# A hybrid block on one core: mixed expert tiles make both up halves first, and the pieces of every turn stand in a new order

## The chip, the cores and the metric

The kernel runs on one core of a Trainium2 chip. The metric is the time of one execution on the device in microseconds, the median of several runs; lower is better. The core's engines are TensorE (PE in the rows; its weight loads are PEld), VectorE (DVE), ScalarE (ACT) and GpSimd (POOL). SyncE (SP) issues most of the transfers, GpSimd issues the rest, and each engine works through its own instruction list in order and waits at semaphores for the others.

## The reference

The input is 16 sequences of 512 tokens with 256 channels. Four residual parts follow one another. Only the shape of the work matters here:

```python
x = x + attn_a(layernorm(x))     # RWKV: time mix, wkv recurrence over 512 steps, channel mix 256-1024-256
x = x + ffn(layernorm(x))        # 8 experts, top 2 of each of 1024 rows: 256-1024-256, gelu
x = x + attn_b(layernorm(x))     # causal conv of 4 taps, two gates, gated recurrence, out product, RMS norm
x = x + ffn(layernorm(x))
...
# in attn_a, on its own layer norms xn and xn2 (mixed with the step before, "lx")
k, v, r = mix_k @ w_key, mix_v @ w_value, mix_r @ w_recept
out = wkv(exp(time_decay), time_first, k, v)                  # log-safe running sums
x = x + out * sigmoid(r) @ w_output
x = x + sigmoid(fmix_r @ f_w_recept) * (square(relu(fmix_k @ f_w_key)) @ f_w_value)
# in ffn
xs = xf[tok]; h = gelu(ragged_dot(xs, w1, tokens_per_expert)); ys = ragged_dot(h, w2, tokens_per_expert)
out = zeros.at[tok].add(ys * w[order][:, None]) + bias
```

The experts take `x.reshape(1024, ...)` in shape only for the scores; only the first 1024 rows of tokens (two sequences) go through them.

## The kernel before

Each of the 16 sequences is a batch of its own, held as 4 chunks of 128 tokens. The program is a row of turns, `turn_first`, `turn_0` to `turn_16`. In turn i batch i is in its time mix (`transposes_in`, `keys`, `value_columns`, `recept_columns`, the scans on VectorE, `outputs`, `transposes_mid`), batch i-1 in its channel mix (8 `channel_key`, 8 `channel_value`, `receptances`), and an earlier one p in its recurrence (`transposes_rec`, `gate_products`, `rec_products`). `ORDER` says which batch the recurrence takes p-th, and `REC_TURN` in which turn. The experts' work is cut into 40 tiles of 128 rows, 20 for each of the two passes; `tile_in`, `tile_up`, gelu and `tile_down` of tile n stand at `TILE_AT` of the turns. 32 tiles have one expert. The other eight (7, 10, 13, 16, 22, 26, 29, 33, `MIXED`) have two experts of 64 rows each. For these TensorE makes the hidden rows with the 64 rows as the weights (`two_up`, L2055, in halves a and b), ScalarE copies them to `hid_rows` (`rows_of_two`, L1155), TensorE turns them over (`two_turn`, L2062), gelu goes over them (`gelu_of`, L1164), and `two_down` (L2071) multiplies by the second weights, two experts at a time. The bank `bank_e` is shared by all of these.

What stands on each engine, and in which order, is written out by hand: each engine has its own functions with the names of the turns, and the calls in them set the order. Turns 5 to 7 share one generic function `turn(i)` on each engine. No scheduler changes this.

Weights of a tile come through SyncE's queue: `load_expert(n)` issues w1 (L482, 1 MB) and w2 (1 MB), with the tile's expert read from `table` into a register (L479), and `load_mixed_w2` issues the four pieces of 512 KB of a mixed tile (L486), two for each half, as its up halves end. The same queue stores finished batches (`store`, L534) and loads new ones (`load_x`, L453). GpSimd's queue carries `keep1` (L669), `keep2` (L685), `keep3` (L706), `residual` (L729) and the indirect transfers `gather` (L755), `picking` (L764) and `scatter_tokens` (L738); between them GpSimd makes the row norms, a power (L638) and a scaling of four chunks (L642): `norm1`, `norm2`, `norm3` of a batch are what `transposes_in`, `transposes_mid` and `transposes_rec` (all L1902) read. Other lines in the rows: L1913 is `channel_key` and `gate_products`, L1992 `channel_value`, L1920 `outputs`, `receptances` and `rec_products`, L1190 the halving of `wo` on ScalarE, L1050 the exponentials of `decay_exps`, L3145 the merge of the experts' rows on VectorE, L3041 and L3051 the last norm of a recurrence, and L3167 its residual sum.

Of the kernel before, what the change touches and what calls it, by code (L numbers as in the profile page):

```python
# [11 lines left out]
B, T, D = 16, 512, 256  # L12
# [136 lines left out]
def hybrid_kernel(nc, x, vecs, bias_row, gamma_row, w_key, w_value, w_recept, w_output, f_w_key, f_w_recept,  # L149
                  f_w_value, w_r_t, w_i_t, w_out_t, expert_weights, expert_indices, w1, w2, out):  # L150
    ctx = ExitStack()
    with ctx:
# [110 lines left out]
        hid_rows = sb("hid_rows", [P, T])  # L263
# [183 lines left out]
        def _(sp):  # L447
# [45 lines left out]
            def load_expert(n):  # L493
# [43 lines left out]
            def load_next(i, place):  # L537
                n = TILE_AT.get((i, place))
                if n in MIXED:
                    load_mixed_w2(n)  # L540
                if n is not None and n + 1 < 2 * NT and (n + 1) % NT:
                    load_expert(n + 1)

            def turn(i):
                late = [p for p in LATE if REC_TURN[p] + 1 == i]
                for b in range(2, B):
                    if i == load_turn(b) and b - NX not in [ORDER[p] for p in late]:
                        load_x(b)
                if i in NORM_TURN:
                    normalised_out(NORM_TURN.index(i))  # L550
                    if NORM_TURN.index(i) == 0:
                        sp.wait_ge(route.sem, route.count(0, "tab"))
                    load_expert(NORM_TURN.index(i) * NT)
                for place in "abcd":
                    load_next(i, place)
                    for p in late if place == "b" else []:
                        store(p)
                        if i == load_turn(ORDER[p] + NX):
                            load_x(ORDER[p] + NX)
                for p in range(B):  # L560
                    if REC_TURN[p] == i < TAIL - 1 and p not in LATE and ORDER[p] >= NB:
                        store(p)

            def tail():
                for place in "abc":
                    load_next(TAIL, place)
                for p in (13, 14, 15):
                    store(p)

            for i in range(0, TAIL):  # L570
                turn(i)
            tail()
# [10 lines left out]
        def _(pool):  # L583
# [195 lines left out]
            def turn_0():  # L779
                norm1(1)  # L780
                keep2(0)
                norm2(0)
                keep1(1)

            def turn_1():
                norm1(2)
                norm2(1)
                keep2(1)
                pool.wait_ge(weights_loaded, 7 * 16)
# [8 lines left out]
            def turn_3():  # L798
                gather(0)
                gather(1)  # L800
                keep2(2)
# [4 lines left out]
                norm2(3)  # L806
                norm3(0)
                next_gather(3, "d")
                keep2(3)
                keep1(4)  # L810

            def turn_4():
                next_gather(4, "a")
                next_gather(4, "b")
                norm1(5)
                next_gather(4, "c")
                gated_input(0)
                norm2(4)
                scaled_input(0)
                keep3(0)  # L820
# [2901 lines left out]
```

## Time and profile before

| | |
|---|---|
| median of 3 runs | 1365.28 us (1363.54 to 1368.07) |
| profiled execution | 1368.03 us, span 1366.0 us |
| TensorE busy | 1219.2 us, 89% of the span, 5812 matmuls |
| VectorE, ScalarE, GpSimd busy | 897.0, 722.5, 595.9 us |
| mean granted clock of TensorE | 0.959 |
| moved | 170.76 MB, mean 125 GB/s |

The span runs from the first to the last instruction of the profiled execution. TensorE is the busiest engine by far, so the time is read from where it stands still and from where its granted clock is below 1.00. Its clock has two levels, 2.4 GHz and 1.2 GHz; a stretch with 0.93 spent part of its time at the lower.

### The profile page before, as it was taken

Reading aid. Unit: us, or ns where it says so; the run is one execution under the profiler, and the core shown is the slowest. Engines: PE = TensorE matmul, PEld = TensorE weight load, DVE = VectorE, ACT = ScalarE, POOL = GpSimd, SP = SyncE. Lnnn points to the kernel's source line nnn. Section 1 sums busy time; section 2 is a strip of 40 time slices with the busy share of each in tenths; the row PEclk is TensorE's granted clock in tenths of the full one; section 3 lists DMA queues with packets and bytes.
Section 4 is the critical chain, followed back from the end, with each engine's and each line's share of the span. In section 5 each row is a group of like instructions: output and inputs, shape, how many; then the busy total and the mean of one; then the engine's idle time right before and its main releaser. Section 6 shows DMA issues by size and latency. Waiting matters only on the chain. (4 is left out here: it accounts for less than half of the span.)

```text
span 1366.0 us, 16873 instructions
## 1 busy us (share of the span) xinstructions
PE 1219.2 (89%) x5812; PEld 944.3 (69%) x5812; DVE 897.0 (66%) x1494; ACT 722.5 (53%) x1116; POOL 595.9 (44%) x529
## 2 busy tenths in 40 slices
PE   4699889999998989889988889899999889999981
PEld 2487677886866858568765758668768578588861
DVE  7989746566675666656879867558656555555344
ACT  3355443654734547346557657547676354463623
POOL 5336554345361443525747536545533512224142
PEclk9899999999999999999999989999999999999996
DMA  8011343547455462464230033666447544644543
GB/s 209 16 32 31 91 114 115 172 144 209 133 162 159 124 182 100 131 193 116 70 89 16 16 108 95 160 168 159 129 135 197 154 125 133 210 112 126 145 123 100
DMA packets 113029, 170.76 MB, mean 125 GB/s; under 512 B 10025, under 2 KB 86577, under 8 KB 112945
## 3 DMA queue, kind: packets, MB, share of 16 engines
q1 hardware_dynamic: 94864, 124.59, 28.6%
q0 software_dynamic: 12320, 39.86, 14.5%
q10 hardware_dynamic: 5760, 5.25, 1.1%
q8 instruction: 46, 0.75, 0.2%
q14 instruction: 39, 0.31, 0.1%
HBM read 138.20 MB, written 16.27 MB: 113 GB/s over the span
## 5 line engine op out<-in xcount | busy, mean ns | idle before, releaser
L638 POOL TENSOR_TENSOR rstd<-varis,half_neg 128x4 f32<-128x4 f32 x64 | 92.7, 1449 | 354.1 <-DVE varis L2814 188.6
L1992 PE MATMUL psum<-fwv,hid 128*128 128x256 f32 x1024 | 240.9, 384 | 0.0
L1992 PEld LDWEIGHTS psum<-fwv,hid 128*128 128x128 f32 x1024 | 194.2, 193 | 29.6 <-issue 3.3
L2033 PEld LDWEIGHTS psum<-xst,ew 128*128 128x128 f32 x1024 | 124.4, 193 | 10.9 <-ACT xst L1151 4.4
L2033 PE MATMUL psum<-xst,ew 128*128 128x128 f32 x1024 | 126.3, 277 | 4.5 <-ACT xst L1151 2.7
L2041 PE MATMUL psum<-ew,hidt 128*128 128x256 f32 x512 | 116.1, 380 | 2.1 <-ACT hidt L1164 2.1
L642 POOL TENSOR_SCALAR xhat<-rows_ring,negmean,rstd 128x256 f32<-128x256 f32 x108 | 107.8, 1009 | 18.3 <-PE psum L1902 11.2
L1064 ACT ACTIVATE hid<-psum 128x512 f32<-128x512 f32 x128 | 75.0, 594 | 71.2 <-PE psum L1913 50.8
L2041 PEld LDWEIGHTS psum<-ew,hidt 128*128 128x128 f32 x512 | 96.5, 190 | 16.8 <-ACT hidt L1164 2.6
L1913 PE MATMUL psum<-xfk_hi,fwk_hi 128*128 128x512 f32 x256 | 90.8, 436 | 8.0 <-ACT hid L1064 4.0
L1164 ACT ACTIVATE hidt<-psum 128x512 f32<-128x512 f32 x80 | 47.8, 597 | 86.8 <-PE psum L2033 79.2
L3008 DVE SCALAR_TENSOR_TENSOR space<-space,vec 128x512 f32<-128x512 f32 x90 | 62.2, 758 | 42.9 <-ACT space L1085 42.8
L1913 PE MATMUL psum<-parts,gw_hi 128*128 128x512 f32 x256 | 76.1, 421 | 15.2 <-ACT space L1105 9.9
L2919 DVE TENSOR_TENSOR_SCAN timely<-dec 128x512 f32<-128x512 f32 x32 | 37.4, 1212 | 69.4 <-ACT dec L1050 69.4
L1913 PE MATMUL psum<-parts,fwk_hi 128*128 128x512 f32 x256 | 80.7, 396 | 0.0
L755 POOL DMA_INDIRECT xs<-xf_rows,token_of_slot x40 | 50.7, 1268 | 67.5 <-PE psum L2021 53.1
L1913 PE MATMUL psum<-xfk_hi,fwk_lo 128*128 128x512 f32 x256 | 80.1, 394 | 0.0
L2827 DVE SCALAR_TENSOR_TENSOR timely<-dec,vec,xn 128x512 f32<-128x512 f32 x96 | 77.6, 866 | 1.9 <-DVE dec L2839 0.5
L1068 ACT ACTIVATE hid<-hid 128x512 f32<-128x512 f32 x128 | 77.5, 628 | 1.6 <-ACT ys L1172 0.8
L1920 PE MATMUL psum<-gwo,space 128*128 128x256 f32 x240 | 58.7, 401 | 21.4 <-DVE space L3036 16.8
L1902 PE MATMUL psum<-ident,xhat 128*128 128x128 f32 x368 | 51.7, 287 | 29.0 <-POOL xhat L642 14.9
L1014 ACT ACTIVATE xn<-psum,vec 128x512 f32<-128x512 f32 x64 | 46.2, 775 | 57.0 <-PE psum L1902 53.2
(299 smaller groups left out, 2597.9 us busy)
## 6 DMA issues: line engine op xcount, KB each, us to landing
ew<-in_w SPq DMA_DIRECT2D x64, 1024.0 KB
ew<-in_w SPq DMA_DIRECT2D x64, 512.0 KB
rows_ring<-bias_rows POOLq DMA_DIRECT2D x28, 512.0 KB, 5.6
rows_ring<-in_x SPq DMA_DIRECT2D x14, 512.0 KB, 4.6
rows_ring<-y POOLq DMA_DIRECT2D x14, 512.0 KB, 6.8
out<-rows_ring SPq DMA_DIRECT2D x14, 512.0 KB, 3.2
rows_ring<-space POOLq DMA_DIRECT2D x12, 512.0 KB, 4.7
ys_rows<-ys ACTq DMA_DIRECT2D x40, 128.0 KB
```

What stands on the lines that cost most here:

```text
L638: pool.tensor_tensor(dst, src, half_neg[:, 0:src.shape[1]], ALU.pow).then_inc(done, 1)
L642: pool.tensor_scalar(dst[:, c, :], src[:, c, :], negmean[n][:, c:c + 1], rstd[n][:, col0 + c:col0 + c + 1], ALU.add, ALU.mult).then_inc(st ...
L1064: nc.scalar.activation(hid[:, j % NHID, :], ring[f"f{j}"], ACT.Relu).then_inc(relu.sem, 1)
L1068: nc.scalar.activation(hid[:, j % NHID, :], hid[:, j % NHID, :], ACT.Square).then_inc(sq.sem, 1)
L1902: last = nc.tensor.transpose(bank_t[:, c, k * P:(k + 1) * P], src[:, k, c * P:(c + 1) * P], ident[:])
L1913: last = nc.tensor.matmul(dst, w[a][:, c, m * P:(m + 1) * P], src[b][:, c, :], start=n == 0, stop=n == len(terms) - 1)
L1920: last = nc.tensor.matmul(dst[:, k, :], src[:, c, k * P:(k + 1) * P], w[:, c, :], start=c == 0, stop=c == chunks - 1)
L1992: last = nc.tensor.matmul(rows4[:, k, :], hid[:, j % NHID, k * P:(k + 1) * P], fwv[:, j, :], start=j == 0 and k % 2 == 0, stop=j == FC - 1 ...
L2033: last = nc.tensor.matmul(bank_e[:, j * P:(j + 1) * P], ew1[:, c, at:at + P], xst[:, c, :], start=c == 0, stop=c == DC - 1)
L2041: last = nc.tensor.matmul(bank_e[:, 0:D], hidt[:, j, :], ew2[:, j, :], start=j == 0, stop=j == FC - 1)
L2827: nc.vector.scalar_tensor_tensor(dst[:, c, :], diff[:, c, :], col(m, c), xn[:, c, 0:T], ALU.mult, ALU.add).then_inc(st.sem, 1)
L3008: nc.vector.scalar_tensor_tensor(s.cv[:, c, :], s.xc[:, c, j:j + T], col(f"conv{j}", c), s.cv[:, c, :], ALU.mult, ALU.add).then_inc(conv.s ...
```

## The change

The pieces of work are the same on every engine, and so are `ORDER`, `REC_TURN`, `TILE_AT` and `MIXED`. Three things differ.

First, `hid_rows` becomes two buffers. TensorE's order at a mixed tile was up a, turn a, up b, turn b, with up b behind gelu a; it becomes up a, up b, turn a, turn b. Up b waits for the copy of half a alone, both turns wait for the copy of half b, and turn b for gelu a too.

Second, SyncE's list is written out turn by turn. `load_expert` is split in `load_first` (w1) and `load_second` (w2), and `load_mixed_w2` in `load_two_w2(n, half)`. The second weights of mixed tiles go ahead of stores, and mostly of loads of x. In a plain tile the expert's number is now read twice, once for each part, and in a mixed one once for each half. At tiles 9 and 20 the second part stands ahead of the first, at tiles 13 and 26 half 1 ahead of half 0.

Third, turns 5 to 7 get lists of their own in place of `turn(i)`, and the calls stand in a new order in all turns, on all five engines. The diff, cut to the functions that change and to some of the lists:

```diff
-        hid_rows = sb("hid_rows", [P, T])
+        hid_rows = [sb(f"hid_rows{n}", [P, T]) for n in range(2)]
...
-            def load_expert(n):
+            def load_first(n):
...
+            def load_second(n):
+                experts = uses(n) if n in MIXED else [expert_in(tile_of(n))]
                 if n:
                     sp.wait_ge(tiles_done, n)
...
-            def load_mixed_w2(n):
+            def load_two_w2(n, half_no):
                 experts = uses(n)
-                for half_no in range(2):
-                    await_step(sp, up, n, "ab"[half_no])
-                    for x, e in enumerate(experts):
-                        load_w2(two_w2[half_no][:, x], e, half_no * FC // 2, FC // 2)
+                await_step(sp, up, n, "ab"[half_no])
+                for x, e in enumerate(experts):
+                    load_w2(two_w2[half_no][:, x], e, half_no * FC // 2, FC // 2)
...
             def rows_of_two(n, half_no):
                 await_step(act, up, n, "ab"[half_no])
-                nc.scalar.activation(hid_rows[:], bank_e, ACT.Copy).then_inc(rows_up.sem, 1)
+                nc.scalar.activation(hid_rows[half_no][:], bank_e, ACT.Copy).then_inc(rows_up.sem, 1)
...
                 if half_no == 0:
                     pe.wait_ge(xst_ready, n + 1)
                 else:
-                    await_step(pe, gelu, n, "a")
+                    await_step(pe, rows_up, MIXED.index(n), "a")
...
             def two_turn(n, half_no):
-                await_step(pe, rows_up, MIXED.index(n), "ab"[half_no])
+                await_step(pe, rows_up, MIXED.index(n), "b")
+                if half_no:
+                    await_step(pe, gelu, n, "a")
```

ScalarE, start: the wait for all late weights and the halving of `wo` move ahead of `values_out(0)` and `decay_exps(0)`.

```diff
-                values_out(0)
-
-            def turn_0():
+
+            def turn_0():
+                act.wait_ge(weights_loaded, 112)
+                nc.scalar.mul(wo[:], wo[:], 0.5).then_inc(split_his, 1)
+                values_out(0)
                 decay_exps(0)
                 weight_exp(0)
                 norm_in(1)
-                act.wait_ge(weights_loaded, 7 * 16)
-                nc.scalar.mul(wo[:], wo[:], 0.5).then_inc(split_his, 1)
```

The next rows are SyncE's instructions around mixed tile 10 (turn 6), before. L482 is the first weights of the tile, L534 a store, L453 a load of x, L479 the reading of expert numbers, L486 the second weights.

```order
106 L482 DMA ew<-in_w 128x2x512
107 L534 DMA out<-rows_ring 128x4x256
108 L453 DMA rows_ring<-in_x 128x4x256
109 L479 TENSOR_LOAD table
110 L479 ISA x2
111 L479 TENSOR_LOAD table
112 L479 ISA x2
113 L486 ISA
114 L486 DMA ew<-in_w 128x4x256
115 L486 ISA
116 L486 DMA ew<-in_w 128x4x256
```

And SyncE at the same place in the changed kernel:

```order
145 L482 DMA ew<-in_w 128x2x512
146 L453 DMA rows_ring<-in_x 128x4x256
147 L479 TENSOR_LOAD table
148 L479 ISA x2
149 L479 TENSOR_LOAD table
150 L479 ISA x2
151 L486 ISA
152 L486 DMA ew<-in_w 128x4x256
153 L486 ISA
154 L486 DMA ew<-in_w 128x4x256
155 L479 TENSOR_LOAD table
156 L479 ISA x2
```

The store has gone from there, the first two transfers of second weights keep the load of x ahead of them, and the expert numbers are read again between the two halves.

GpSimd in turn 3, before. L755 gathers an expert tile's rows, L685 is `keep2(2)`, L638 with L642 are norms, L669 is `keep1(3)`; the `xhat` row at the end is `norm1(4)`.

```order
51 L744 TENSOR_TENSOR rstd<-varis,half_neg 128x8
52 L755 DMA xs<-xf_rows,token_of_slot 128x256 x2
53 L685 DMA rows_ring<-y 128x1024
54 L638 TENSOR_TENSOR rstd<-varis,half_neg 128x4
55 L642 TENSOR_SCALAR y<-rows_ring,negmean,rstd 128x256 x4
56 L669 DMA rows_ring<-bias_rows 128x1024
57 L638 TENSOR_TENSOR rstd<-varis,half_neg 128x4
58 L642 TENSOR_SCALAR xhat<-rows_ring,negmean,rstd 128x256 x4
```

GpSimd at the same place in the changed kernel:

```order
51 L894 TENSOR_TENSOR rstd<-varis,half_neg 128x8
52 L835 DMA rows_ring<-y 128x1024
53 L905 DMA xs<-xf_rows,token_of_slot 128x256 x2
54 L788 TENSOR_TENSOR rstd<-varis,half_neg 128x4
55 L792 TENSOR_SCALAR y<-rows_ring,negmean,rstd 128x256 x4
56 L819 DMA rows_ring<-bias_rows 128x1024
57 L788 TENSOR_TENSOR rstd<-varis,half_neg 128x4
58 L792 TENSOR_SCALAR xhat<-rows_ring,negmean,rstd 128x256 x4
```

`keep2(2)` now stands ahead of the two gathers; the rest is as it was.

Five more places of which the prediction speaks:

- GpSimd, turn 9: before `norm1(10)`, `picking(0, 0)`, `picking(0, 1)`, `norm3(5)`; now `picking(0, 1)` stands behind `norm3(5)`.
- GpSimd, turn 11: before `norm3(8)`, `gather(NT + 1)`, the gathers of places b and c, `keep3(7)`, `residual(7)`; now `keep3(7)` stands ahead of `norm3(8)`, and `residual(7)` ahead of the gather of place c.
- ScalarE, turn 8: before `relu_of(7, 0)` stands behind `weight_exp(8)`, now 14 calls ahead of it.
- TensorE: before `transposes_mid` of the batch stands right ahead of `rec_products` in turns 5 to 7 with nothing between them; now other work of 1.7 to 5.2 us of TensorE stands between.
- VectorE, last turn: before all 16 instructions of the merge at the end, behind `residual(15)`; now 8 of them (`merge(1, 0)`) between `recur(15)` and `mean_square(15)`.

## Rows read from the trace of the kernel before

**Rows 1.** The page, busy time by engine: us, share of the span, instructions.

```profile
PE 1219.2 (89%) x5812; PEld 944.3 (69%) x5812; DVE 897.0 (66%) x1494; ACT 722.5 (53%) x1116; POOL 595.9 (44%) x529
```

**Rows 2.** Waits of PE: total us, number of waits, longest us.

```profile
PE psum L2071 <- DMA ew<-in_w: 16.3, 5, 4.1
PE psum L1902 <- POOL xhat L642: 14.9, 7, 4.3
...
PE psum L1920 <- ACT xn L1014: 4.6, 3, 1.5
```

**Rows 3.** Stretches: length, busy us by engine, granted clock, DMA share, GB/s.

```profile
188.00:210.00 22.00, 17.85 (x89) 15.47 (x88) 11.29 (x20) 5.47 (x9) 8.58 (x5) 0.84 0.29 90
210.00:377.00 167.00, 164.46 (x856) 131.72 (x854) 105.23 (x164) 93.69 (x144) 73.00 (x60) 1.00 0.52 155
410.00:435.00 25.00, 20.57 (x109) 15.55 (x108) 10.28 (x13) 12.06 (x16) 0.43 (x1) 0.93 0.60 172
586.00:606.00 20.00, 15.88 (x91) 11.86 (x90) 12.18 (x14) 11.43 (x15) 4.51 (x4) 0.91 0.67 204
683.00:710.00 27.00, 21.78 (x91) 17.77 (x90) 19.39 (x35) 12.99 (x22) 9.91 (x12) 0.87 0.45 112
710.00:795.00 85.00, 74.51 (x305) 56.16 (x304) 70.24 (x112) 57.77 (x87) 52.29 (x37) 0.94 0.07 13
860.00:885.00 25.00, 19.84 (x81) 14.84 (x80) 9.03 (x17) 13.39 (x18) 12.82 (x12) 0.86 0.62 173
```

**Rows 4.** Timeline of 399:423, SP's queue and PE: start, us, what, idle before.

```profile
401.33 0.39 SPq L534 DMA_DIRECT2D out<-rows_ring  x1
...
404.44 3.62 SPq L486 DMA_DIRECT2D ew<-in_w  x4
...
405.01 1.94 PE L2055 MATMUL psum<-ew,xst 128*64 128x512 f32 x8
...
419.56 3.01 PE L2071 MATMUL psum<-ew,hidt 128*64 128x256 f32 x16 [3.85 <-DMA ew<-in_w]
```

**Rows 5.** Timeline of POOL, 162:193.

```profile
162.59 1.47 POOL L755 DMA_INDIRECT xs<-xf_rows,token_of_slot  x1 [7.95 <-DMA xf_rows<-ew]
...
165.78 1.04 POOL L685 DMA_DIRECT2D rows_ring<-y  x1
...
176.38 2.18 POOL L642 TENSOR_SCALAR y<-rows_ring,negmean,rstd 128x256 f32<-128x256 f32 x4 [0.22 <-POOL rstd L638]
...
183.23 9.13 POOL L642 TENSOR_SCALAR xhat<-rows_ring,negmean,rstd 128x256 f32<-128x256 f32 x4 [0.20 <-issue]
```

**Rows 6.** Timeline of POOL, 661:690.

```profile
661.70 1.12 POOL L764 DMA_INDIRECT ew<-ys_rows,slot_i  x1 [0.18 <-issue]
...
685.57 1.21 POOL L638 TENSOR_TENSOR rstd<-varis,half_neg 128x4 f32<-128x4 f32 x1
```

**Rows 7.** Timeline of POOL, 860:863.

```profile
861.11 0.89 POOL L729 DMA_DIRECT2D rows_ring<-space  x1 [5.04 <-issue]
```

**Rows 8.** Timeline of PE, 862:870.

```profile
866.48 2.08 PE L1913 MATMUL psum<-parts,gw_hi 128*128 128x512 f32 x4 [5.16 <-ACT space L1105]
```

**Rows 9.** Timeline of DVE, 1343:1366.

```profile
1352.55 0.17 DVE L3041 TENSOR_SCALAR msq<-ssq 128x4 f32<-128x4 f32 x1 [7.77 <-ACT square L1144]
...
1356.06 7.41 DVE L3145 SCALAR_TENSOR_TENSOR xf<-ew,choice_w,xf 128x256 f32<-128x256 f32 x16
```

**Rows 10.** Timeline of ACT, 27:30.

```profile
27.49 1.91 ACT L1050 ACTIVATE dec<-dec 128x2048 f32<-128x2048 f32 x1 [0.77 <-DVE dec L2914]
```

**Rows 11.** Timeline of SP's queue, 15:19.

```profile
17.02 0.72 SPq L473 DMA_DIRECT2D choice_w<-in_expert_weights  x1
```

**Rows 12.** DMA issues: transfer, KB, median us to landing.

```profile
choice_w<-in_expert_weights SPq DMA_DIRECT2D x1, 8.0 KB, 11.7
```

**Rows 13.** Timeline of PE, 40:50.

```profile
43.91 5.82 PE L1920 MATMUL psum<-wo,dec 128*128 128x256 f32 x16 [13.52 <-DVE dec L2955]
```

**Rows 14.** Critical chain, 1263:1265: start, us, step.

```profile
1263.19 1.40 PE psum L1913 x6
```

More of the change, by code:

```diff
@@ L535, in store @@
                     .then_inc(out_stored[without_experts(p) % 3], 16)
[L537 to L572, printed above, removed]
+            def turn_first():
+                pass
+            def turn_0():
+                load_x(2)
+            def turn_1():
+                pass
+            def turn_2():
+                load_x(4)
+                load_x(3)
+            def turn_3():
+                load_x(5)
+                normalised_out(0)
+                sp.wait_ge(route.sem, route.count(0, "tab"))
+                load_first(0 * NT)
+                load_second(0 * NT)
+                load_first(1)
+                load_second(1)
+                load_first(2)
+                load_second(2)
+                load_first(3)
+                load_second(3)
@@ L573, in _ @@
+            turn_first()
+            turn_0()
+            turn_1()
+            turn_2()
+            turn_3()
+            turn_4()
+            turn_5()
+            turn_6()
+            turn_7()
+            turn_8()
+            turn_9()
+            turn_10()
+            turn_11()
+            turn_12()
+            turn_13()
+            turn_14()
+            turn_15()
+            turn_16()
             for b in range(NB):
@@ new lines, in turn_6, with turn_7 @@
+            def turn_6():
+                keep3(2)
+                norm1(7)
+                gated_input(2)
+                scaled_input(2)
+                keep2(6)
+                norm2(6)
+                next_gather(6, "b")
+                keep1(7)
+                norm3(3)
+                mean_power(2)
+                next_gather(6, "c")
+            def turn_7():
+                norm1(8)
+                residual(2)
+                next_gather(7, "a")
+                gated_input(3)
+                scaled_input(3)
+                keep2(7)
+                norm2(7)
+                next_gather(7, "b")
+                next_gather(7, "c")
+                norm3(4)
+                keep3(3)
+                mean_power(3)
+                residual(3)
+                keep1(8)
@@ L987, in _ @@
             turn_4()
-            for i in range(5, 8):
-                turn(i)
+            turn_5()
+            turn_6()
+            turn_7()
             turn_8()
@@ L1882, in _ @@
             turn_4()
-            for i in range(5, 8):
-                turn(i)
+            turn_5()
+            turn_6()
+            turn_7()
             turn_8()
@@ L2759, in _ @@
             turn_4()
-            for i in range(5, 8):
-                turn(i)
+            turn_5()
+            turn_6()
+            turn_7()
             turn_8()
@@ L3674, in _ @@
             turn_4()
-            for i in range(5, 8):
-                turn(i)
+            turn_5()
+            turn_6()
+            turn_7()
             turn_8()
```

1924 lines of the change are left out of this document (1153 added, 771 removed).

## The prediction

> **What bounds the kernel now.** I read the page first. TensorE is busy 1219.2 of 1366 us [rows 1]; no other engine comes near, so the kernel loses time where TensorE stands still (147 us in all) and where its granted clock falls. Then the table of its waits: the largest named kinds that this change touches are second weights not landed (16.3 us in 5 waits), row norms from GpSimd (14.9 in 7), and copies of `xn` on ScalarE (4.6 in 3) [rows 2]. Then stretches of time, cut at the waits of 3 us and more. From 210 to 377 TensorE is busy 164.46 of 167 us at clock 1.00, so there an order has nothing to give. Right behind the waits the clock is not full: 0.84, 0.93, 0.91, 0.87, 0.86 [rows 3]. So each wait is paid twice, itself and then (1 - clock) times its stretch: 3.5 us in 188:210, 1.8 in 410:435, 1.8 in 586:606, 3.5 in 683:710, 3.5 in 860:885. The mean clock of 0.959 over the span makes that 56 us in all. Last, the timelines around each wait, to see what came last.
>
> **The change part by part.** All pieces of work stay, so what can change is waits and the clock behind them. I write the sum against the profiled execution, 1368.0 us; the median of the runs shown is 2.7 lower.
>
> *A, second weights of mixed tiles.* At tile 10 the four transfers are issued from 404.44 over 3.62 us, behind a store at 401.33 and a load of x, and TensorE starts the second half of `two_down` at 419.56 after 3.85 us of waiting [rows 4]. Between issue and landing lie 15.1 us, in which some 2.6 MB move at the stretch's 172 GB/s: these second weights (2 MB) and the load of x. Now the store is gone from there, so the queue is free some 3 us earlier, and half 0 no longer shares its wait with half 1; the last byte would land near 401.5 + 15.1 = 416.6. On TensorE, between the end of up b and `two_down` stood 6.7 us of work (two pieces of `channel_key` at 1.40 [rows 14], the turn, `receptances`); now both turns, a product of the time mix, a piece more of `channel_key` and the transposes of a middle norm stand there, 12.9 us counted from the order. That need not make `two_down` later; it makes up b earlier. So its second half wants its weights at 419.56 - 3.85 = 415.7 at the earliest, and 417.4 with the extra piece ahead: the wait goes, by a margin of only 1 us. The other mixed tiles gain alike (6.7 to 12.5 at tile 7, 6.7 to 11.1 at 13, 1.7 to 8.0 at 29, 2.7 to 7.7 at 33). Full worth: 16.3 plus four stretches like 410:435 at 1.8 of clock, 23.5. Lower bound 0, if the landing doesn't move; I take 18.
>
> *B, GpSimd in turn 3.* `keep2(2)` is issued at 165.78, behind two gathers of which the first waited 7.95 us for the experts' rows. So the norm behind it starts only at 176.38 and `norm1(4)`'s scaling at 183.23, where it takes 9.13 us [rows 5]; TensorE waits for it, idle 4.15 of 22 us with 3.5 of clock (17.85 busy at 0.84) [rows 3]. Now `keep2(2)` is ahead of the gathers. What is late next is the `y` norm's own operands, which have been there for long. -7.5.
>
> *C, GpSimd in turn 9.* 16 indirect transfers from 661.70 to 685.57 stand ahead of `norm3(5)` [rows 6], and TensorE stands idle for it, 27 less 21.78 or 5.2 us, and loses 3.5 of clock behind [rows 3], 8.7. Eight of the 16 now stand behind it, 12 us earlier. I take 6, since the middle norm and `keep2(9)` are behind those eight.
>
> *D, GpSimd in turn 11.* `residual(7)` is issued at 861.11 after 5.04 us of waiting for the transfer ahead of it [rows 7]; ScalarE's tanh of the gates waits for its landing, TensorE for the tanh, 5.16 us [rows 8], and 3.5 of clock. Now `keep3(7)` is ahead of `norm3(8)` and `residual(7)` ahead of the third gather: over 6 us earlier. -8.5.
>
> *E, ScalarE in turn 8.* `relu_of(7, 0)` behind `weight_exp(8)`: 20 us with 15.88 busy and 1.8 of clock [rows 3]. Now 14 calls earlier. -5.9.
>
> *F, middle transposes.* `rec_products` right behind `transposes_mid` waits for the copy of `xn` that empties its bank, 4.6 us in 3 waits [rows 2]. Now work of 1.7 to 5.2 us lies between. -4.6.
>
> *G, the end.* VectorE stands idle 7.77 us before 1352.55, and then has a merge of 16 instructions, 7.41 us, as the last compute [rows 9]. Eight of them (3.7 us) now fit into that idle time. -3.7.
>
> *H, the start.* ScalarE's `decay_exps(0)` ran at 27.49 [rows 10]. Now the wait for all late weights stands ahead, whose last transfer is issued at 17.02 [rows 11] and takes 11.7 us to land [rows 12]: that is 28.7, and with the halving of `wo` and the values' copy (0.6 each) the exponentials start near 30.3. Scans follow from there up to `outputs(0)`, which already waits 13.52 us for them [rows 13]. Between 0 and +3; I take +2.4.
>
> *I, new waits.* The middle transposes of batch 10 already wait, the longest of the seven (4.3) [rows 2], and stand 2.4 us of work nearer to `outputs(10)`. Gates of batches 5 to 7 stand 1.6 nearer to the products that need them; tile 9's first weights go behind its second (+1); the expert numbers are read twice on SyncE, which is idle then. +5, between 0 and 15.
>
> The sum of the named parts is -18 - 7.5 - 6 - 8.5 - 5.9 - 4.6 - 3.7 + 2.4 + 5 = -46.8. Not all of it will stay. These are chains over four engines, and where one wait goes, the next late piece shows; from 710 to 795 TensorE has 10.5 us idle and 5.1 of clock with no wait above 4.3 [rows 2, 3], which is how a tight order looks once the great waits are gone. I keep two thirds: -31, so 1337 in the profile's terms, **1334.5 as the median**.
>
> **Two rules weighed.** From 410 to 435 the DMA engines are busy 0.60 of the time [rows 3]. So they aren't full on average, and moving a store out of the way frees the queue more than the engines. The Trainium skill, page "DMA: Bandwidth & Descriptors", section "Issuing engines are not separate DMA queues", says that transfers of all issuers run on the same 16 engines and interleave; by it an earlier issue only spreads the same bytes, and A would be worth little. The trace half agrees: 0.60 busy leaves room, 15.1 us for 2.6 MB does not look like it.
>
> Four scalings by GpSimd took 2.18 us at 176.38 and 9.13 at 183.23, the same instruction on the same shapes [rows 5]. So a norm's price depends on what runs beside it. The Trainium skill, page "SBUF — State Buffer", section "A bandwidth-pool intuition that's wrong (but worth ruling out)", says that GpSimd and a VectorE operation on two ports exclude one another, one fully blocked; by that the slow scaling follows VectorE's place in the order, and a new order moves it at random.
>
> **The rivals.**
> - *Bandwidth.* Second weights land no earlier. For: 15.1 us from issue to landing at 172 GB/s, and the margin of 1 us in A. Against: 0.60 busy. A is worth 6 in place of 18, the sum -34.8, two thirds of it -23: 1345 profiled, 1342 as the median (1336 to 1350). 0.20.
> - *Nearly all is kept.* Each wait was alone in its chain. The sum itself, -47: 1321 profiled, 1318 (1311 to 1322). For: 210:377 shows that an order can run at 98% [rows 3]. 0.16.
> - *Slower: norms on GpSimd come late in the new order.* Each one that TensorE waits for costs up to 4.3 [rows 2] and some 1.8 of clock, 6.1 together. Seven did before. Against the 31 us kept it decides from five more on; seven more make +43, 1368 + 12 = 1380 profiled, 1377. For: 9.13 against 2.18, and 16 batches have three norms each. Against: B, C and D free that engine of waits. 0.13.
> - *No change.* New waits eat all that the named ones give: within 4.1 us of 1365.3. 0.08.
>
> **How the numbers follow.** The likeliest case (0.43) has its own range of 1322 to 1346. Three tenths of a per cent, 4.1 us, is about what can be told from no change. Faster: 0.43 + 0.20 + 0.16 = 0.79; same 0.08; slower 0.13. The range for 8 in 10 leaves out half of the case where nearly all is kept and the slower one: 1315 to 1364.
>
> **What the profile after would show.** A: second weights under 5 us in TensorE's waits, and full clock behind the mixed tiles; if the wait is there with the transfers issued 3 us earlier, bandwidth was the cause. B, C, D: the waits at `transposes_in(4)`, `transposes_rec(5)` and `gate_products(8)` gone; busy share in the matching stretches above 97%. G: no more than four us of merge behind the last residual sum. H: `outputs(0)` starting near 46.5. TensorE's busy time itself should fall from 1219 by 15 to 20 us, as the clock is full for longer; the mean clock near 0.97. The prediction is wrong if new waits of 3 us and more stand where none were, above all for norms from GpSimd with scalings of 6 to 9 us.

## The result and the profile after

| | before | changed |
|---|---|---|
| median | 1364.41 us (1362.59 to 1368.07, 4 runs) | 1284.51 us (1283.05 to 1289.51, 4 runs) |
| span of the profiled execution | 1366.0 us | 1281.0 us |
| mean granted clock | 0.959 | 0.979 |

The ratio is 0.9418 (95% interval 0.9385 to 0.9451): faster by 79 us, where 31 were forecast. The time lies below the range, which began at 1315.

The page of the changed kernel, head and busy times:

```profile
span 1281.0 us, 17105 instructions
...
PE 1194.1 (93%) x5812; PEld 932.4 (73%) x5812; DVE 889.7 (69%) x1494; ACT 717.9 (56%) x1116; POOL 606.5 (47%) x529
```

Against [rows 1] TensorE is busy 25 us less with the same 5812 matmuls, which is the clock, and stands idle 87 in place of 147 us. (1 - clock) times the span is 56.0 before and 26.9 after. So of the 85 us of span 60 are waits, and 25 of busy time is speed (29 by the difference of the two clock products).

TensorE's waits by releaser, the kinds that answer to [rows 2] (L2182 is L1902 of before, L2193 L1913, L2313 L2033, L2321 L2041):

```profile
PE psum L2182 <- POOL xhat L792: 13.0, 7, 3.4
...
PE psum L2321 <- DMA ew<-in_w: 2.2, 1, 2.2
...
PE psum L2313 <- DMA ew<-in_w: 0.8, 1, 0.8
PE psum L2193 <- ACT hid L1243: 0.8, 1, 0.8
...
PE psum L2193 <- ACT space L1284: 0.5, 1, 0.5
```

Not one wait at `two_down` (L2353) is left of the 16.3 us. In their place stand small ones at plain tiles. The copies of `xn` no longer appear at all. Norms from GpSimd still cost 13.0 in 7, and not at the same places.

Stretches, cut where the same pieces now lie, to hold against [rows 3]:

```profile
184.00:206.00 22.00, 19.29 (x103) 17.08 (x102) 12.84 (x22) 10.08 (x15) 8.68 (x7) 0.92 0.37 114
229.00:604.00 375.00, 372.97 (x1922) 293.59 (x1922) 249.75 (x400) 215.75 (x339) 171.00 (x143) 1.00 0.58 166
395.00:420.00 25.00, 25.00 (x151) 20.68 (x150) 17.60 (x29) 15.30 (x23) 9.65 (x10) 1.00 0.62 158
545.00:565.00 20.00, 20.00 (x115) 14.61 (x114) 13.35 (x26) 14.57 (x22) 7.63 (x9) 1.00 0.88 236
641.00:668.00 27.00, 26.22 (x121) 21.67 (x119) 23.43 (x44) 18.40 (x27) 20.80 (x19) 1.00 0.29 75
668.00:753.00 85.00, 73.61 (x300) 54.79 (x300) 78.17 (x120) 59.04 (x89) 52.94 (x37) 0.96 0.10 19
803.00:828.00 25.00, 25.00 (x126) 19.90 (x125) 16.80 (x29) 15.68 (x23) 7.94 (x6) 1.00 0.54 162
```

The first is `transposes_in(4)`: 19.29 in place of 17.85 busy. The second shows the reach of the new order: 375 us of turns 4 to 8 with two us of TensorE idle. The next two are tile 10 and turn 8, full at clock 1.00, even with the DMA engines 0.88 busy at 236 GB/s. Then turn 9; then turn 10, which is idle for as long as it was (73.61 of 85 busy, 74.51 before); then turn 11, full.

Tile 10, SyncE's queue and TensorE, against [rows 4]:

```profile
383.21 1.94 PE L2335 MATMUL psum<-ew,xst 128*64 128x512 f32 x8
...
385.34 6.45 SPq L486 DMA_DIRECT2D ew<-in_w  x4
...
388.71 1.94 PE L2335 MATMUL psum<-ew,xst 128*64 128x512 f32 x8
...
403.54 3.67 PE L2353 MATMUL psum<-ew,hidt 128*64 128x256 f32 x32
```

The second weights are issued from 385.34 over 6.45 us, the last of them after up b at 388.71, and `two_down` runs 32 matmuls in 3.67 us without a break.

GpSimd in turn 3, against [rows 5]:

```profile
152.88 1.00 POOL L835 DMA_DIRECT2D rows_ring<-y  x1
...
168.56 2.18 POOL L792 TENSOR_SCALAR y<-rows_ring,negmean,rstd 128x256 f32<-128x256 f32 x4 [0.22 <-POOL rstd L788]
...
180.69 7.22 POOL L792 TENSOR_SCALAR xhat<-rows_ring,negmean,rstd 128x256 f32<-128x256 f32 x4 [0.20 <-issue]
```

`keep2(2)` is 13 us ahead and the `y` norm 8, but the `xhat` scaling for batch 4 only 2.5 us earlier, at 180.69: it waits for its own statistics now. 2.7 of TensorE's 4.15 us stay in this profile. The size of this one wait moves between profiles of kernels with the same lists there: 1.6 in three later runs, 2.7 in three.

The end, VectorE, against [rows 9]:

```profile
1262.82 3.76 DVE L3524 SCALAR_TENSOR_TENSOR xf<-ew,choice_w,xf 128x256 f32<-128x256 f32 x8
1270.93 0.17 DVE L3420 TENSOR_SCALAR msq<-ssq 128x4 f32<-128x4 f32 x1 [4.36 <-ACT square L1323]
...
1274.45 3.75 DVE L3524 SCALAR_TENSOR_TENSOR xf<-ew,choice_w,xf 128x256 f32<-128x256 f32 x8
```

Half the merge (3.76) lies in front of the last norm, and idle time there is down from 7.77 to 4.36. The start, against [rows 13]:

```profile
45.88 4.49 PE L2200 MATMUL psum<-wo,dec 128*128 128x256 f32 x13 [13.52 <-DVE dec L3334]
```

`outputs(0)` starts 2.0 us later, as step H said.

### The profile page after: what moved, and what is told of

Read it like the earlier page. It is cut to its first block and busy times, and to the rows that moved or that the text cites. A ratio compares the mean times of both kernels' runs of the same rounds, so it can differ in the third digit from the quotient of the medians.

```text
span 1281.0 us, 17105 instructions
## 1 busy us (share of the span) xinstructions
PE 1194.1 (93%) x5812; PEld 932.4 (73%) x5812; DVE 889.7 (69%) x1494; ACT 717.9 (56%) x1116; POOL 606.5 (47%) x529
## 3 DMA queue, kind: packets, MB, share of 16 engines
q10 hardware_dynamic: 5760, 5.25, 1.2%
## 5 line engine op out<-in xcount | busy, mean ns | idle before, releaser
L788 POOL TENSOR_TENSOR rstd<-varis,half_neg 128x4 f32<-128x4 f32 x64 | 97.1, 1518 | 246.4 <-DVE varis L3193 178.1
L2313 PEld LDWEIGHTS psum<-xst,ew 128*128 128x128 f32 x1024 | 125.8, 194 | 8.2 <-issue 3.6
L792 POOL TENSOR_SCALAR xhat<-rows_ring,negmean,rstd 128x256 f32<-128x256 f32 x108 | 122.2, 1141 | 16.5 <-PE psum L2182 9.6
L2313 PE MATMUL psum<-xst,ew 128*128 128x128 f32 x1024 | 126.6, 277 | 1.4 <-DMA ew<-in_w 0.8
L2321 PE MATMUL psum<-ew,hidt 128*128 128x256 f32 x512 | 117.6, 383 | 2.9 <-DMA ew<-in_w 2.2
L2321 PEld LDWEIGHTS psum<-ew,hidt 128*128 128x128 f32 x512 | 98.0, 192 | 18.4 <-issue 3.8
L2193 PE MATMUL psum<-xfk_hi,fwk_hi 128*128 128x512 f32 x256 | 94.6, 451 | 1.8 <-ACT timely L1221 1.8
L905 POOL DMA_INDIRECT xs<-xf_rows,token_of_slot x40 | 45.4, 1134 | 92.0 <-PE psum L2301 73.1
L2193 PE MATMUL psum<-parts,fwk_hi 128*128 128x512 f32 x256 | 80.7, 396 | 0.0
L2193 PE MATMUL psum<-xfk_hi,fwk_lo 128*128 128x512 f32 x256 | 80.2, 395 | 0.0
L863 POOL TENSOR_TENSOR space<-space 128x1024 f32<-128x1024 f32 x14 | 33.3, 2379 | 88.4 <-ACT space L1294 88.4
L2182 PE MATMUL psum<-ident,xhat 128*128 128x128 f32 x368 | 50.4, 282 | 26.2 <-POOL xhat L792 13.0
L3206 DVE SCALAR_TENSOR_TENSOR timely<-dec,vec,xn 128x512 f32<-128x512 f32 x96 | 73.8, 822 | 1.5 <-DVE dec L3218 0.5
L2193 PE MATMUL psum<-parts,gw_hi 128*128 128x512 f32 x256 | 71.9, 403 | 1.3 <-ACT hid L1243 0.8
L2200 PE MATMUL psum<-wo,dec 128*128 128x256 f32 x256 | 59.5, 386 | 13.7 <-DVE dec L3334 13.5
L2182 PEld LDWEIGHTS psum<-ident,xhat 128*128 128x128 f32 x368 | 43.1, 144 | 37.4 <-issue 32.5
```

The source lines that it names most:

```text
L788: pool.tensor_tensor(dst, src, half_neg[:, 0:src.shape[1]], ALU.pow).then_inc(done, 1)
L792: pool.tensor_scalar(dst[:, c, :], src[:, c, :], negmean[n][:, c:c + 1], rstd[n][:, col0 + c:col0 + c + 1], ALU.add, ALU.mult).then_inc(st ...
L2182: last = nc.tensor.transpose(bank_t[:, c, k * P:(k + 1) * P], src[:, k, c * P:(c + 1) * P], ident[:])
L2193: last = nc.tensor.matmul(dst, w[a][:, c, m * P:(m + 1) * P], src[b][:, c, :], start=n == 0, stop=n == len(terms) - 1)
L2200: last = nc.tensor.matmul(dst[:, k, :], src[:, c, k * P:(k + 1) * P], w[:, c, :], start=c == 0, stop=c == chunks - 1)
L2313: last = nc.tensor.matmul(bank_e[:, j * P:(j + 1) * P], ew1[:, c, at:at + P], xst[:, c, :], start=c == 0, stop=c == DC - 1)
```

## The experiments

Two theories were held against each other in most of them. *Every wait stands alone*: TensorE's next late piece depends on work near by, so a wait that is taken away comes back in full, with its clock, and later ones keep their sizes. *Waits are passed on*: TensorE then comes early to the next piece, and part of the gain is given back. The second was the reason for keeping two thirds in the forecast. Times are given as ratios to the kernel before, which ran beside each; "slower than the changed kernel" means the difference of such a ratio and 0.9418, in us, and is good to 6 or 7 us.

**The mixed tiles alone** (kernel before, with up b and turn a changing places, and the queue's order; ScalarE copies half b to its buffer ahead of gelu a, and the tiles from 16 on are changed in the same way):

```diff
-                two_turn(a, 0)
+                two_up(a, 1)
                 ...
-                two_up(a, 1)
+                two_turn(a, 0)
```

and in SyncE's list, at the head of its `turn(i)`, which serves turns 0 to 15 on this engine (the store's old place at the end goes):

```diff
+                if TILE_AT.get((i, "a")) in MIXED:
+                    load_mixed_w2(TILE_AT[i, "a"])
+                for p in range(B):
+                    if REC_TURN[p] == i - 1 and p not in LATE and ORDER[p] >= NB:
+                        store(p)
```

> The kernel before, with the mixed tiles alone changed: both up halves first in two buffers, and in SyncE's queue the second weights of the mixed tile at the head of a turn ahead of the pending store and the load of x. Theory 'every wait stands alone': 16.3 us of weight waits and four times 1.8 of clock come back, 1341 to 1345 from 1364.4, and the waits behind keep their sizes. Theory 'waits are passed on': TensorE comes earlier to the next late piece, and two thirds or less of it stays, 1349 to 1356. Theory 'bandwidth': the second weights land no earlier, the waits stay above 10 us, 1358 or more.

Measured 1347.01 us, ratio 0.9853 (0.9814 to 0.9892): 20 us. From 1364.4 that is 1344.3, in the first theory's range; the interval reaches to the edge of the second's. No wait for second weights at `two_down` is left. Three of the waits that had nothing to do with the edit, as they stand in this kernel's table (two lines later in the file):

```profile
PE psum L1904 <- POOL xhat L644: 14.7, 7, 4.1
...
PE psum L1904 <- POOL hidt L644: 5.2, 1, 5.2
PE psum L1922 <- ACT xn L1016: 4.6, 3, 1.5
```

14.7, 5.2 and 4.6, as in the kernel before (14.9, 5.2 and 4.6). Only small new ones at the second turn (1.26 us, three times, for gelu) took something back. The waits speak for the first theory.

**The queue's order alone** (the second half of that diff, without the first):

> The kernel before with SyncE's order alone changed: second weights of the mixed tile at the head of a turn first, then the store, then x. If the queue's order is the cause of the weight waits: most of the 20 us of both parts together, 1346 to 1351. If the two up halves next to each other are: 1358 or more.

Ratio 0.9967 (0.9945 to 0.9989): 4.5 us. Tile 10 in its timeline:

```profile
399.54 7.73 SPq L486 DMA_DIRECT2D ew<-in_w  x4
...
404.23 1.94 PE L2057 MATMUL psum<-ew,xst 128*64 128x512 f32 x8
...
407.31 0.51 SPq L534 DMA_DIRECT2D out<-rows_ring  x1
...
418.56 3.44 PE L2073 MATMUL psum<-ew,hidt 128*64 128x256 f32 x16 [3.63 <-DMA ew<-in_w]
```

The store now stands behind the weights, half 0 is issued 4.9 us earlier than in [rows 4], and TensorE still waits 3.63 for half 1, as half 1 can only be issued after up b (404.23). It was up b's place that set the issue, not the store. Step A of the prediction had the wrong link here, with the right total. In the mixed tiles alone up b ends at the same time, but `two_down` starts 2.7 us further behind it (416.46 for 413.76), and there is no wait.

**The order of up and turn undone in the changed kernel** (the first half of the diff, backwards):

> The changed kernel with up b behind gelu a again (up a, turn a, up b, turn b), all other places as they are. By the order the work between up b and two_down falls by about 1.3 us at most. Theory 'the swap is what helps': TensorE waits again at up b or at two_down, 6 us or more, 1291 or more. Theory 'the placing of other work and the queue help, the swap hardly': within 3 us of 1284.5.

1291.71 us, ratio 0.9453 (0.9415 to 0.9491), 4.8 us by the ratios, though the two intervals overlap. The time lies at the edge of the first theory's range, its sign does not show: the profile has weight waits of 1.95 and 1.31 us back, at tiles 22 and 26, and none at 10 or 13. With the other work placed in front of `two_down`, most tiles don't need the two halves next to each other.

**Three moves on GpSimd alone** (B, C and D in the kernel before):

```diff
+                keep2(2)
                 gather(0)
                 gather(1)
-                keep2(2)
...
-                picking(0, 1)
                 norm3(5)
+                picking(0, 1)
...
+                keep3(7)
                 norm3(8)
                 gather(NT + 1)
                 next_gather(11, "b")
+                residual(7)
                 next_gather(11, "c")
-                keep3(7)
-                residual(7)
```

> The kernel before, with three moves on GpSimd alone: keep2(2) ahead of the gathers in turn 3, picking(0, 1) behind norm3(5) in turn 9, keep3(7) and residual(7) forward in turn 11. Theory 'every wait stands alone': 7.5 + 8.7 + 8.5 less what stays at transposes_in(4) (2.7 in the changed kernel) gives 22, 1342 to 1346. Theory 'waits are passed on': 10 to 15 us, 1350 to 1355, with new waits within some 30 us behind each place.

1351.57 us, ratio 0.9884 (0.9846 to 0.9921): 16 us, less than the first theory's 22. The waits at `transposes_in(4)` and `gate_products(8)` are gone; at `transposes_rec(5)` 4.1 of 5.2 us stay. GpSimd shows why:

```profile
672.97 1.95 POOL L638 TENSOR_TENSOR rstd<-varis,half_neg 128x4 f32<-128x4 f32 x1 [6.18 <-DVE varis L2814]
675.12 7.05 POOL L642 TENSOR_SCALAR hidt<-xf,negmean,rstd 128x256 f32<-128x256 f32 x4 [0.20 <-issue]
```

With the picks out of the way the norm waits 6.18 us for VectorE's statistics, and its scaling takes 7.05 us, where it took 2.27 behind the picks. VectorE is busy for 6.46 of the 7.1 us, and was for 0.2 of the 2.2. B and D came in full, C did not, and little was passed on: behind the start, every other wait of 0.3 us and more stayed within half a microsecond but for one at the second weights of tile 29, which fell from 4.13 to 2.75.

**The same three undone in the changed kernel:**

> The changed kernel with the same three GpSimd moves undone. Theory 'every wait stands alone': +17 to +22, 1302 to 1307. Theory 'waits are passed on' (a kernel freed of its waits is the more sensitive): other waits appear too, over +22. Theory 'the other lists made these moves needless': under +8.

1299.53 us, ratio 0.9502 (0.9467 to 0.9536), 11.5 us by the ratios and 16.6 by the spans. The first is in none of the three ranges, the second just under the first of them, so this run decides nothing between the theories. `transposes_in(4)` waits 7.9 us (2.7 with the moves), `gate_products(8)` 5.4, and undoing C brings a wait at another place:

```profile
650.05 1.22 PE L2193 MATMUL psum<-xfk_hi,fwk_hi 128*128 128x512 f32 x2 [4.28 <-ACT hid L1243]
```

This is `channel_key(8, 4)`. So a move may keep a different wait away than the one that it had removed in the old order.

**The last turn alone** (lists of TensorE, ScalarE and VectorE for turn 16 from the changed kernel):

> The kernel before, with the last turn alone as in the changed kernel on TensorE, ScalarE and VectorE (rec_products(14) ahead of expert tile 38, transposes_rec(15) ahead of the second half of up of tile 39, half the merge ahead of mean_square(15)). The prediction priced only the merge, 3.7 us. 'Every wait stands alone': the merge's 3 to 3.7, and the wait of 5.25 at gate_products(15) with its clock, 8 to 12 in all, 1352 to 1356 beside 1364. If only the merge counts: 1360 to 1361.

1357.07 us, ratio 0.9939 (0.9917 to 0.9961): 8.3 us. The wait of 5.25 at `gate_products(15)` is gone, and 2.7 for weights at the last tile is new.

**The last turn undone in the changed kernel:**

> The changed kernel with the last turn of TensorE, ScalarE and VectorE as before. The last turn alone gave 0.6 per cent, 8.3 us, in the kernel before. 'Every wait stands alone': +8 to +11, 1293 to 1296, with gate_products(15) waiting 5 us again. 'Passed on': under +5.

1288.23 us, ratio 0.9439 (0.9405 to 0.9472): 2.9 us by the ratios and 4.2 by the spans: under 5, as 'passed on' had it. The 5.24 are back, but the 2.2 for weights at tile 39 are gone with it.

**All named parts together, and two more moves** (`weight_exp(8)` behind `relu_of(7, 0)`, `rec_products(p)` behind `keys(i + 1)` in turns 5 to 7):

> The kernel before with everything of the earlier single runs together (mixed tiles and queue, three GpSimd moves, the last turn) and two more: weight_exp(8) behind relu_of(7, 0) on ScalarE, rec_products behind keys(i + 1) in turns 5 to 7. 'Every wait stands alone': the ratios multiply, 0.985 x 0.988 x the tail's, and 5 + 4 us for the last two, so 1305 to 1312. 'Waits are passed on': 1320 or more, with waits in places where the single runs had none.

1329.18 us, ratio 0.9722 (0.9682 to 0.9762): 38 us. The three single parts multiply to 0.968, 44 us, so the two more moves gave nothing, or took up to 6 (which the intervals don't tell from nothing), where 9 had been expected. The time lies in the range of 'waits are passed on'. In the profile the three waits of 1.54 at `rec_products` are gone, and `transposes_rec(4)`, behind them, waits 5.1 us for VectorE where it had waited 1.8, and `value_columns` waits 0.64 twice; `channel_key(7, 3)` still waits 2.6 of 3.5. Here a move made by hand on one engine, without the others' lists being fitted to it, was passed on. `channel_key(2, 0)`, far from both, waits 4.3 for 1.8, for which the trace names no releaser. It does so in the run of the last turn alone too, where `transposes_in(4)` behind it waits 2.4 less, so it belongs to neither move; what makes it vary stays open.

**The two halves of the program.** The lists of all engines and the queue were cut at turn 9: the changed ones in front and those of before behind, and the other way round. Two pieces and a load of x that had crossed the cut were put back.

> The changed kernel up to turn 8, and the lists of the kernel before from turn 9 on, on all engines and the queue (mixed tiles 22, 26, 29, 33 in the old order of up and turn). In the profiles outputs(9) starts 45 us earlier in the changed kernel, the rest comes behind. If the two halves of the program add: 1320 to 1324, and the waits behind turn 9 as in the kernel before, to 0.3 us. If late lists lose what early ones gave: 1330 or more.

1336.9 us, ratio 0.9796 (0.9759 to 0.9833): 28 us, and in the range that had been given to the rival. The profile in two stretches:

```profile
229.00:603.00 374.00, 372.11 (x1916) 292.70 (x1914) 249.17 (x400) 215.57 (x339) 169.14 (x143) 1.00 0.57 164
603.00:1300.00 697.00, 637.49 (x3047) 500.79 (x3048) 442.58 (x725) 392.82 (x617) 307.41 (x262) 0.96 0.44 122
```

Up to 603 it is the changed kernel, with 1.9 us idle from 229 on; behind, it has the waits of before, `gate_products(8)` 5.26, `rec_products(11)` 3.68, `receptances(14)` 1.82, beside one of 6.4 at the cut itself, at `transposes_in(10)`. The cut lies between `outputs(8)` and `outputs(9)`. From the one to the other, first in the kernel before, then here:

```profile
628.00:699.90 71.90, 66.48 (x307) 52.96 (x306) 55.25 (x92) 35.41 (x57) 45.42 (x41) 0.95 0.40 105
587.40:670.60 83.20, 72.24 (x315) 57.93 (x314) 55.34 (x94) 38.26 (x59) 47.26 (x41) 0.92 0.34 89
```

At `outputs(8)` this kernel is 40.6 us ahead of the kernel before (the changed one 39.7), at `outputs(9)` only 29.3. So the 11 us were lost at the cut, and behind it, from `outputs(9)` to the end, it takes 663.8 us, where the kernel before took 666.2: the late lists of before lost nothing of what the early ones gave.

> The other half: the kernel before up to turn 8, the changed lists from turn 9 on. If the halves add: 1365 less 80 plus 43, 1326 to 1331. If the early lists are a condition for the late ones: 1340 or more.

1319.66 us, ratio 0.9665 (0.9631 to 0.9699): 46 us, and 6 us under the range. Neither run hit its range, since 45 us had been put in front of the cut, where 40 lie, and nothing had been put down for the seam. The product of the two ratios is 0.9468, the ratio of the whole change 0.9418. By the spans the halves give 31.7 and 47.3 us, 79.0 of 85.1. So the halves add, but for 6 or 7 us that the seam costs.

**One engine's whole list undone.** What was open by then was which list carried the rest of the gain.

> The changed kernel with the whole list of GpSimd as in the kernel before; the other engines and the queue as changed. The three moves alone, undone, cost 11 us. If the rest of GpSimd's new order matters little: 1296 to 1300. If each engine's list carries its share of the small waits: 1305 or more.

1329.17 us, ratio 0.9738 (0.9703 to 0.9773): 44 us slower than the changed kernel. Waits for norms grow (7.3 at `transposes_in(4)`, 6.0 at `transposes_mid(12)`, 4.9 at `transposes_in(14)`, 4.6 at `transposes_rec(5)`), and 5.2 us at the second weights of tile 13.

> The changed kernel with SyncE's whole list as in the kernel before (stores and loads of x ahead of the second weights of mixed tiles). The queue's order alone gave 4.5 us in the kernel before. If the work that now lies between up b and two_down covers the late landing by itself: under +4, no wait at two_down. If not: 16 us of weight waits and their clock are back, 1300 or more.

1320.37 us, ratio 0.9671 (0.964 to 0.9703): 35 us slower than the changed kernel. TensorE's wait for second weights:

```profile
PE psum L2203 <- DMA ew<-in_w: 33.8, 8, 11.5
```

And why, at tile 10, GpSimd and SyncE's queue:

```profile
395.45 1.24 POOL L729 DMA_DIRECT2D rows_ring<-space  x1
...
403.20 0.39 SPq L534 DMA_DIRECT2D out<-rows_ring  x1
...
406.48 2.48 SPq L486 DMA_DIRECT2D ew<-in_w  x4
```

The store at 403.20 waits for the landing of `residual`, which GpSimd issues at 395.45, and load of x and second weights wait behind it, to 406.48. `two_down(10)` then stands 11.5 us. In the kernel before `residual` stood at 396.67 and the first second weights at 404.44, hardly otherwise. But there up b ended at 406.95, so half 1 could not be issued before; here up b ends at 389.57, both halves could be issued from then on, and TensorE wants them from 402.5 on. In the kernel before the queue's order cost 4.5 us. In the new order the whole old list costs 35.

**The start put back** (changed kernel, on ScalarE):

```diff
-                act.wait_ge(weights_loaded, 112)
-                nc.scalar.mul(wo[:], wo[:], 0.5).then_inc(split_his, 1)
                 values_out(0)
                 ...
                 norm_in(1)
+                act.wait_ge(weights_loaded, 112)
+                nc.scalar.mul(wo[:], wo[:], 0.5).then_inc(split_his, 1)
```

> The changed kernel with the start of ScalarE as before: the wait for the late weights and the halving of wo behind norm_in(1). The chain decay_exps(0) to outputs(0) is shorter by about 2 us and is what TensorE waits for (13.5), so 2 us faster, 1282 to 1283. If the load of the late weights is what counts: no difference.

1278.78 us, ratio 0.9373 (0.9343 to 0.9403). `outputs(0)` starts at 43.59 for 45.88. The 2.3 us are the start's; the rest of the distance in the medians is within what two sets of runs differ by.

**Three waits of middle norms covered by one piece each:**

> The changed kernel with the start of ScalarE as before, and on TensorE three of the waits that are left (transposes_mid(8), (10) and (12), 2.1, 2.9 and 3.4 us) each covered by one piece of 1.7 us that stood behind. 'Every wait stands alone': 1.7 us less at each and some clock, 5 to 7 us under the version with the start put back, near 1273. 'Passed on': the same time, since the next product waits for the norms behind the transposes.

1279.83 us, ratio 0.9364 (0.9341 to 0.9387): the same. `transposes_mid(12)` in it, TensorE:

```profile
892.34 1.07 PE L2182 MATMUL psum<-ident,xhat 128*128 128x128 f32 x8 [1.35 <-POOL xhat L792]
895.83 0.66 PE L2301 MATMUL psum<-ident,xs 128*128 128x128 f32 x2 [2.42 <-ACT ys L1351]
...
909.07 1.99 PE L2272 MATMUL psum<-fwv,hid 128*128 128x256 f32 x8 [1.82 <-ACT hid L1247]
```

Its wait fell from 3.4 to 1.35, and 2.42 came at `tile_in(25)` and 1.82 at the next `channel_value`. Passed on, as in the two hand moves above.

## Why the prediction was wrong

**What bounds the kernel** and the double price of a wait were right: beside 60 us less idle time the clock gave 25 to 29, nearly half as much again, and the 39 us of named waits had been priced with 19.5 of clock.

**A** was taken at 18 and measured 20 alone, and all weight waits went. Its mechanism was half right. In the old order the second half's issue hung on up b, not on the store; in the new one the queue decides, as the queue list of before costs 35 us there. The working from 15.1 us and 172 GB/s was off too: that rate is the mean of 410:435, and between issue and landing the engines moved 284 GB/s (below). **B** went to 0 in the old order with the one move, but in the changed kernel 2.7 of 4.15 stay, as the norm's own statistics are late next. **C** was right in the changed kernel, where the wait is gone, but the move alone gave 1 us of 5.2; it named the picks, and VectorE's statistics and a slow scaling came last right behind them. **D** held in full. **E** and **F** are gone in the changed kernel, but the one move that the prediction named for each took F's waits away only to bring another of the same size, and E's by a quarter. **G** measured 3.2 from `rec_products(15)` to the end, for 3.7. **H** was right to 0.4 us. **I** was too small in waits: new or larger ones stand at `transposes_mid(12)` 3.4, `transposes_rec(7)` 3.1, `tile_down(39)` 2.2, `transposes_mid(8)` 2.1 and `channel_key(10, 1)` 1.8 (0.7 in seven of the later runs with the same turn). The sign that was to tell that the prediction is wrong, new waits of 3 us and more, is there twice, and the kernel is faster than forecast all the same.

**The step that failed first is the sum.** It came to 47, and the span fell by 85. Even with nothing taken off it, the forecast would have been 1318, and 1284.5 lies far below that. It priced the waits that had a name, most of them of 3 us and more. Taking off start and end (30.0 and 13.0 us), the waits of 0.3 us and more at single pieces make 88 us in the kernel before, and of these the named ones 39. The other 49 stood at zero. Four of them, at `recept_columns(10)`, `gate_products(7)`, `rec_products(11)` and `gate_products(15)`:

```profile
726.92 2.40 PE L1907 MATMUL psum<-timely,wr 128*128 128x512 f32 x3 [3.20 <-ACT timely L1037]
...
800.09 1.22 PE L1913 MATMUL psum<-parts,gw_hi 128*128 128x512 f32 x2 [3.11 <-ACT space L1105]
...
1067.73 1.84 PE L1920 MATMUL psum<-gwo,space 128*128 128x256 f32 x6 [3.79 <-DVE space L3036]
...
1324.21 2.08 PE L1913 MATMUL psum<-parts,gw_hi 128*128 128x512 f32 x4 [5.25 <-DVE parts L2835]
```

A fifth, 4.3 at `transposes_mid(10)`, the prediction knew, as a wait that might grow, and thirty more lie between 0.3 and 3. After the change 30 us of 88 are left: 2.7 of the named 39, and 27 that are either left of the 49 or new. So the named places lost 36 us of waits, and the others 22 on balance, each with its clock. The row of turn 10, which the prediction took as the picture of a tight order, was that of one turn only; it has stayed as it was, while from 828 to 1240 TensorE is busy 403.67 of 412 us, near the 98% of 210:377.

**The second step that failed is the one from the sum to the forecast**: "I keep two thirds", 16 us. In the changed kernel 36 of the 39 us of named waits went, the two halves of the program add up to all but 7 us, and parts A, B and D and the last turn, each alone, left nearly all other waits where they were. Against that stand edits on a few lists: C, E, F, the last turn undone and the last experiment, where half or more of what was expected did not show in the time. All the named parts made by hand gave 38 us, of 54 for A to G, which is two thirds indeed. So the discount fitted named moves made one by one, and was put on a change of all lists, in which the pieces that would have been late next had been moved as well. That it was the fitting of all lists together which kept the rest from being passed on is argued from these runs, and no run shows it by itself.

**The rivals.** *Bandwidth* is refuted as a forecast: it had A at 6 us, and the mixed tiles alone gave 20 and left no wait for second weights. But what spoke against it, 0.60 busy, was misread. That is the mean from 410 to 435, most of which lies behind the landing. From the issue of tile 10's second weights to their landing in the kernel before, and from their issue to `two_down` in the changed one:

```profile
404.40:419.60 15.20, 11.35 (x65) 7.63 (x63) 11.08 (x15) 6.64 (x12) 5.42 (x5) 1.00 1.03 284
385.30:403.50 18.20, 18.20 (x74) 11.21 (x73) 15.97 (x32) 8.59 (x16) 17.39 (x16) 1.00 0.70 176
```

The DMA engines were full in the first (1.03, since packets are counted where they start). The last of the four transfers was issued by 408.1 and had landed by 419.6, 11.5 us later, while TensorE wanted it after 7.7. In the changed kernel it is issued by 391.8, 11.7 us of other work stand in front of `two_down`, and its half is wanted only behind the 16 matmuls of half 0. So it was the distance from issue to need that took the wait away; the engines had no room in the old order. The Trainium skill, page "DMA: Bandwidth & Descriptors", section "Issuing engines are not separate DMA queues", says that the transfers of all issuers share 16 engines and interleave; that agrees with the 1.03. What delayed the weights by another 21 us in the run with the old queue list was a place in SyncE's list (issue at 406.48 in place of 385.34), ahead of the engines. *"Nearly all is kept"* was nearer, with too small a sum: its range ended at 1311. The *slower* one had a true core: norms still cost 13.0 in 7, and the scaling in front of `transposes_in(4)` takes 7.22 us, but at no more places than before. The long scalings follow VectorE: in the kernel before it was busy for none of the 2.18 us and for 8.97 of the 9.13 us in [rows 5].

**Open:** which of the lists of TensorE, ScalarE and VectorE carries what. No run puts one of the three back alone. The runs show that GpSimd's list is worth 44 and the queue's 35 us in the presence of the rest, but such a run prices the misfit of an old list with new ones too, and the 44 and 35 together would already make up all of the 79, so these shares don't say how the 79 divide; alone in the old order what was tried of the two gave 16 and 4.5.

## What to carry to other kernels

Sum every wait of the bounding engine, the small ones too, before deciding what a change of a whole order can give; the named few were under half here. Discount a gain for being passed on when one list is edited and the others are not; when all lists are refitted, this one case speaks for pricing the sum as it stands. And look into each in-order queue for a transfer that waits for something slow ahead of one that is urgent: stores in front of second weights cost 4.5 us in one order, and 35 in another, in which TensorE's up halves had been done for 17 us when the weights were issued. Read how busy the DMA engines are from issue to landing, and not over a stretch that goes on behind it: 1.03 and 0.60 in the same place.

## What the runs showed that had not been expected

The DMA engines were 0.88 busy at 236 GB/s over 20 us without delaying TensorE. A wait's price in clock is large and comes with it: taking 13 us of waits from the mixed tiles took 21 us from the span, and the mean clock went from 0.959 to 0.966. Waits far from an edit repeat from kernel to kernel to a tenth of a microsecond in most places (1.54 at `rec_products` of turns 5 to 7 in the six kernels that keep these lists there, 13.02 to 13.07 in front of the last `rec_products` in all sixteen), so the wait table can be read piece by piece as a fingerprint of an order. A few don't: `transposes_in(4)` with `channel_key(2, 0)`, `recept_columns(10)` (2.4 or 3.0 with the changed lists) and `channel_key(10, 1)` (0.7 or 1.8), so one such wait in one profile proves little.
